# Gated weight tables kept in 32 bit and merged by one 32-bit product per block, with the splitting of their shares taken out of the first phase

## The reference

```python
gh = relu(einsum('bsd,hd->bsh', x, gfc1_w) + gfc1_b)
g = (einsum('bsh,eh->bse', gh, gfc2_w) + gfc2_b).mean(axis=1)     # 16 batches x 8 gates
W1m = W1 + einsum('be,efd->bfd', g, tv_W1)                        # tv_W1: 8 x 512 x 128
W2m = W2 + einsum('be,edf->bdf', g, tv_W2)                        # tv_W2: 8 x 128 x 512
h = relu(einsum('bsd,bfd->bsf', x, W1m) + b1m[:, None, :])
out = einsum('bsf,bdf->bsd', h, W2m) + b2m[:, None, :]
```

## Time and profile before

| | |
|---|---|
| median of three runs | 747.9 us |
| profiled execution, its own time | 749.55 us |
| span of its trace | 747.8 us |
| busy PE / PEld / DVE / ACT / POOL | 93% / 71% / 88% / 87% / 62% |
| matmuls | 12002 |
| mean granted clock of TensorE | 0.975 of full |
| first phase, loop part | about 70 to 440 us |
| blocks 0 to 7, 8 to 15, second group | 482 to 494, 496 to 505, 607 to 621 us |

### The profile page before, as it was taken

One profiled execution on the slowest core, in us unless ns is written; L12 is line 12 of the kernel. 1 busy time (PEld: TensorE's weight loads), 2 busy tenths in 40 slices (PEclk: granted clock), 3 DMA queues, 4 the chain that ended last, 5 costly groups with the idle time before them and its releaser, 6 DMA issues. The chain is left out here.

```text
span 747.8 us, 38168 instructions
## 1 busy us (share of the span) xinstructions
PE 692.5 (93%) x12002; PEld 533.8 (71%) x12002; DVE 659.1 (88%) x2409; ACT 649.1 (87%) x1780; POOL 465.2 (62%) x790
## 2 busy tenths in 40 slices
PE   4898899999999999999999999888999998999993
PEld 2576677777777777777777777775777787777772
DVE  5697889999999999999999999768898977998983
ACT  4797989999999999999999999557888876888883
POOL 3686778888888888888888888421333321333333
PEclk9798999999999999999999999899999999999998
DMA  4757676666666666666666666410222211222221
GB/s 149 112 110 134 132 129 129 148 143 131 148 142 132 148 141 132 148 141 134 148 139 135 148 142 123 74 51 1 73 85 83 71 58 31 85 70 84 84 84 70
DMA packets 202485, 82.66 MB, mean 111 GB/s; under 512 B 176093, under 2 KB 189824, under 8 KB 202377
## 3 DMA queue, kind: packets, MB, share of 16 engines
q1 hardware_dynamic: 202440, 82.08, 48.3%
HBM read 22.79 MB, written 17.30 MB: 54 GB/s over the span
## 5 line engine op out<-in xcount | busy, mean ns | idle before, releaser
L892 DVE SCALAR_TENSOR_TENSOR scores_lo<-p_a,scores_hi 128x512 f16<-128x512 f32 x256 | 173.3, 683 | 1.7 <-ACT scores_hi L786 1.3
L786 ACT ACTIVATE scores_hi<-p_a 128x512 f16<-128x512 f32 x256 | 156.2, 611 | 9.3 <-PE p_a L623 9.3
L1010 POOL CAST qk_parts<-qk_f 128x512 f16<-128x512 f32 x128 | 78.0, 610 | 50.2 <-issue 24.9
L1442 POOL TENSOR_TENSOR ffn_rstd_shift<-ffn_rstd_shift,consts 128x4 f32<-128x4 f32 x32 | 36.5, 1142 | 109.1 <-DVE ffn_rstd_shift L1400 109.1
L984 POOL TENSOR_TENSOR stats<-stats,consts 128x2 f32<-128x2 f32 (+1 forms) x128 | 88.2, 689 | 17.9 <-DVE stats L925 13.1
L1224 PE MATMUL psb<-merged_W_of_batch,h_hi 128*128 128x128 f16 x512 | 94.5, 220 | 2.2 <-DVE h_lo L1378 1.5
L1378 DVE TENSOR_TENSOR h_lo<-h_f,h_hi 128x512 f16<-128x512 f32 x128 | 95.6, 786 | 1.1 <-ACT h_hi L1280 1.1
L1269 ACT ACTIVATE h_f<-psb,merged_b_of_batch 128x512 f32<-128x512 f32 x128 | 87.2, 709 | 10.3 <-PE psb L1205 8.6
L1225 PE MATMUL psb<-merged_W_of_batch,h_hi 128*128 128x128 f16 x512 | 94.2, 220 | 0.0
L1226 PE MATMUL psb<-merged_W_of_batch,h_lo 128*128 128x128 f16 x512 | 94.1, 220 | 0.0
L1016 POOL TENSOR_TENSOR qk_parts<-qk_f,qk_parts 128x256 f16<-128x256 f32 x128 | 85.9, 671 | 10.2
(11 more groups left out here) (215 smaller groups left out, 2697.5 us busy)
## 6 DMA issues: line engine op xcount, KB each, us to landing
x_f<-in_x SPq DMA_DIRECT2D x32, 256.0 KB, 3.2
t_rows<-t SPq DMA_DIRECT2D x64, 128.0 KB, 1.8
t_back<-t_rows SPq DMA_DIRECT2D x32, 256.0 KB, 2.6
out<-out_tile SPq DMA_DIRECT2D x32, 256.0 KB, 2.1
tv_share<-in_L_ffn_tv_W SPq DMA_DIRECT2D x32, 128.0 KB, 2.2
qkT_parts<-qk_parts SPq DMA_TRANSPOSE x128, 3.1
zT_hi_lo<-z_parts SPq DMA_TRANSPOSE x128, 2.3
merged_W<-in_L_ffn_W SPq DMA_DIRECT2D x2, 256.0 KB, 4.4
```

The costliest lines, as they stand in the source:

```text
L786: nc.scalar.activation(ah[:, t % 2, cols], p_a[:, cols], ACT.Relu).then_inc(ahi_ready[eo], 1)
L892: nc.vector.scalar_tensor_tensor(al[:, t % 2, cols], p_a[:, cols], 0.0, ah[:, t % 2, cols], ALU.max, ALU.subtract).then_inc(alo_ready[eo], 1)
```

## The change

The two 16-bit halves of the tables become one 32-bit table `tv`. SP loads the shares straight to their place in it, both at t = 1 and without a wait. The stages `tv_hi` and `tv_lo` go. The gates are kept in 32 bit only, with the scale WS moved into the constant `delta`. Of the four products per output the three with table parts become one with 32-bit operands. Besides, `VECTOR_ORDER` has `stats2` ahead of `v_lo` and `mean_var2`, `mean_var1` ahead of `state_lo`, and `GPSIMD_ORDER` has `split_x` ahead of `z_hi`.

```diff
-                ("exp_qk", 1), ("state_hi", 3), ("v_hi", 1), ("tv_hi", 0), ("scores_hi_0", 4), ("copy_out", 6),
+                ("exp_qk", 1), ("state_hi", 3), ("v_hi", 1), ("scores_hi_0", 4), ("copy_out", 6),
-GPSIMD_ORDER = [("rsqrt", 1), ("z_hi", 10), ("split_x", 0), ("z_lo", 10), ("qk_hi", 2), ("qk_lo", 2),
+GPSIMD_ORDER = [("rsqrt", 1), ("split_x", 0), ("z_hi", 10), ("z_lo", 10), ("qk_hi", 2), ("qk_lo", 2),
...
-        tv = [sb(top, f"tv_{s}", [P, 2, FO * C], F16) for s in ("hi", "lo")]
+        tv = sb(top, "tv", [P, 2, FO * C])
...
-                        if t not in (1, 5) or isinstance(b, int) and b + 1 == B:
-                            return
-                        which = t // 4
-                        sp.wait_ge(ones_set, 1)
-                        sp.wait_ge(tv_split, TVP * b + TVP // 2 * (which + 1))
-                        tv_rows(b + 1, which)
...
+                        if t != 1 or isinstance(b, int) and b + 1 == B:
+                            return
+                        tv_rows(b + 1)
+
+                    def tv_rows(b):
+                        cols = bass.ds(b * TVW, TVW)
+                        for i, src in enumerate((d["L1_ffn_tv_W1"].rearrange("e (i o) d -> (e i) (o d)", i=FI),
+                                                 d["L1_ffn_tv_W2"].rearrange("e (i o) f -> (e i) (o f)", i=FI))):
+                            sp.dma_start(tv[:, i, cols], src[:, cols]).then_inc(tv_loaded, 16)
...
-                            mm(o, th, gh, start=True, stop=False)
-                            mm(o, th, gl, start=False, stop=False)
-                            mm(o, tl, gh, start=False, stop=False)
+                            mm(o, tv[:, 0, c0:c0 + P], g, start=True, stop=False)
                             last = mm(o, w1s[:, c0:c0 + P], delta2h[:, :, :].rearrange("p b i -> p (b i)"),
                                       start=False, stop=True)
...
-                        link(nc.vector.tensor_tensor(gbf[:, :, :], kcol("delta").unsqueeze(1).broadcast_to([P, GB, FI]),
-                                                     grep[:, GB:B].unsqueeze(2).broadcast_to([P, GB, FI]), ALU.mult))
-                        link(nc.vector.tensor_copy(gbh[:, GB:B, :], gbf[:, :, :]))
-                        nc.vector.tensor_tensor(gbl[:, GB:B, :], gbf[:, :, :], gbh[:, GB:B, :], ALU.subtract)\
+                        nc.vector.tensor_tensor(gb[:, GB:B, :], kcol("delta").unsqueeze(1).broadcast_to([P, GB, FI]),
+                                                grep[:, GB:B].unsqueeze(2).broadcast_to([P, GB, FI]), ALU.mult)\
                             .then_inc(gb_ready, 1)
```

More of the change, by code:

```diff
@@ L170, in build @@
         grep = sb(top, "gate_by_row", [P, B])
[L171 to L173 removed]
+        gb = sb(top, "gate_blocks", [P, B, FI])
         bw = wm1p[:, 1, 0:4 * BW].bitcast(F32).rearrange("p (i w) -> p i w", i=2)
@@ L420, in build @@
             qk_turned, z_turned = [[sem(f"{s}_{i}") for i in range(4)] for s in ("qk_turned", "z_turned")]
-            tv_loaded = [sem(f"tv_loaded_{i}") for i in range(2)]
-            tv_hi_ready, tv_split = sem("tv_hi_ready"), sem("tv_split")
+            tv_loaded = sem("tv_loaded")
             def at_least(eng, s, value):
@@ L508, in store @@
                             .then_inc(t1_stored[pair], 16)
-                    for which in range(2):
-                        tv_rows(0, which)
+                    tv_rows(0)
                     sp.wait_ge(base_stored, 32)
@@ L696, in merge_w1 @@
                             pe.wait_ge(base_placed, 16 * 4)
-                            pe.wait_ge(tv_split, TVP * B)
+                            pe.wait_ge(tv_loaded, 32 * B)
                             pe.wait_ge(gb0_ready, 1)
@@ L700, in merge_w1 @@
                             pe.wait_ge(mlo_ready, k - 1)
-                        gh, gl = [x[:, 0:GB, :].rearrange("p b i -> p (b i)") for x in (gbh, gbl)]
+                        g = gb[:, 0:GB, :].rearrange("p b i -> p (b i)")
                         for j in range(4):
@@ L731, in split_x @@
                         nc.scalar.activation(xh[:, hf, cols], xf[:, hf, cols], ACT.Copy).then_inc(xh_ready, 1)
-                    def tv_hi(b, t):
-                        if t % 2:
-                            return
[L736 to L741, removed]
                     def read_t1(b, t):
@@ L823, in merged_w1_hi @@
                             .then_inc(mhi_ready, 1)
-                    run(act, SCALAR_ORDER, {"tv_hi": tv_hi, "split_x": split_x, "read_t1": read_t1, "v_hi": v_hi,
+                    run(act, SCALAR_ORDER, {"split_x": split_x, "read_t1": read_t1, "v_hi": v_hi,
                         "exp_qk": exp_qk, "relu_qk": relu_qk,
@@ L842, in mean_var1 @@
                         nc.vector.bn_aggr(st[:, t % 4, MEAN:MEAN + 2], st[:, t % 4, 0:9]).then_inc(mv1, 1)
[L844 to L852, removed]
                     def v_lo(b, t):
@@ L964, in merged_w1 @@
                         nc.vector.tensor_tensor(lo, src, hi, ALU.subtract).then_inc(mlo_ready, 1)
-                    run(dve, VECTOR_ORDER, {"tv_lo": tv_lo, "stats1": stats1, "mean_var1": mean_var1, "v_lo": v_lo,
+                    run(dve, VECTOR_ORDER, {"stats1": stats1, "mean_var1": mean_var1, "v_lo": v_lo,
                         "make_qk": make_qk, "shift2": shift2, "state_lo": state_lo,
@@ L1181, in merge @@
                                     c0 = (4 * i + j) * C
-                                    th, tl, base = tv[0][:, 0, :], tv[1][:, 0, :], w1s
+                                    rows, base = tv[:, 0, :], w1s
                                 else:
                                     c0 = (4 * (i % 2) + j) * F + (i // 2) * P
-                                    th, tl, base = tv[0][:, 1, :], tv[1][:, 1, :], w2s
+                                    rows, base = tv[:, 1, :], w2s
                                 o = ps[:, merge_bank(g, k), j * P:(j + 1) * P]
-                                gh, gl = (x[:, g * GB:(g + 1) * GB, :].rearrange("p b i -> p (b i)")
-                                          for x in (gbh, gbl))
-                                mm(o, th[:, c0:c0 + P], gh, start=True, stop=False)
-                                mm(o, th[:, c0:c0 + P], gl, start=False, stop=False)
-                                mm(o, tl[:, c0:c0 + P], gh, start=False, stop=False)
+                                mm(o, rows[:, c0:c0 + P], gb[:, g * GB:(g + 1) * GB, :].rearrange("p b i -> p (b i)"),
+                                   start=True, stop=False)
                                 last = mm(o, base[:, c0:c0 + P], delta2h[:, :, :].rearrange("p b i -> p (b i)"),
```

22 lines of the change are left out of this document (5 added, 17 removed).

## The result

The kernel took 757.0 us after the change (median of 12 runs, 753.3 to 759.5), against 748.8 us before (12 runs, 745.7 to 751.7) on the same chip: 1.0100 times the time before, 95% interval 1.0077 to 1.0123. The forecast was 757 us: the same time, but from three runs of the kernel before with a median of 747.9 us; the forecast change was +9.1 us and the measured one is +8.2. The profiled span went from 747.8 to 754.9 us.

A forecast was written before the change was run, and what follows sets the result against it. SP's queue was taken to bound the first phase and PE the second group's merging. The terms 7.1 + 3.0 + 1.0 - 1.0 - 1.0 gave +9.1 us, 757 us; the range to hold 8 in 10 was 750 to 763 us.

The forecast's parts named there:

- What bounds the kernel: First phase: SP's queue, never waiting from 132 to 440 us, sets the 28 us turn; PE paces the second group's merging.
- Rival A: First phase: ACT and DVE set the pace, so removing tv_lo gains 22 us, giving 737 us; chance 0.06.
- Second group, +7.1 us: Merging of 16 blocks, paced by PE: 0.44 us more per block with the 32-bit product, all on the path.
- sixth unit: Merged output: L669's row gives 0.33 us, one unit beyond the five counted from the skill page (0.28 us), origin unknown.
- Blocks 8 to 15, +3.0 us: Merging of these eight blocks: +3.5 us for the product, less for two DVE gate steps of 0.23 + 0.29 us.
- Drain, +1.0 us: Blocks 0 to 7: +1.5 us for the product, partly filling PE's waits, less 0.5 us for two gate steps.
- the splits at the ends, -1.0 us: Ramp and drain: removing tv_hi and tv_lo gains 1 us, at most 6.7; nothing counts from 132 to 440 us.
- SP's queue, -1.0 us: SP's loads of table shares: between 0.1 us less and 0.15 us more each, -2.2 to +3.3 us over 11 batches.
- Rival D: Loads with both ends worked out at run time hold SP +0.3 us each, 8 us in all, 765 us; chance 0.05.
- The orders, 0: DVE's and POOL's changed orders give nothing under SP's pace, between -1 and +1 us at the ends.
- B: Rival: the 32-bit product is hidden, the merging adds under 2 us, no change at 748 us; chance 0.10.
- C: Rival: the merging costs more, 0.17 us per output (768 us) or 0.11 with nothing hidden (761 us); chance 0.09.

The follow-up runs named there:

- e4: Kernel after, with both tables loaded once by two 2 MB transfers that ScalarE issues ahead of the first phase: 752.1 us, ratio 1.0062.
- e5: Kernel before, with t1 stored once per half batch instead of twice, two SP issues fewer a turn: 747.3 us, ratio 0.9990.
- e10: Kernel after, with four 16-bit base products per output (tables' and gates' share left out) and t1 stored once per half batch: 732.5 us, ratio 0.9784.
- e12: Kernel before, with t1 stored once per half batch and ScalarE's tv_hi left out, upper halves cleared once: 747.2 us, ratio 0.9990.
- e8: Kernel after, with t1 stored once per half batch and the tables in eight 512 KB transfers from ScalarE: 745.8 us, ratio 0.9966.
- e6: Kernel after, with t1 stored once per half batch instead of twice: 742.8 us, ratio 0.9930.
- e7: Kernel after, with each merged block's four 32-bit products made first, then its four 16-bit base products: 751.0 us, ratio 1.0050.
- e3: Kernel before with all its splits, each output's three 16-bit table products replaced by one 32-bit product of constants: 760.3 us, ratio 1.0169.
- e2: Kernel after, with each merged output made by four 16-bit base products, the tables' and gates' share left out: 744.7 us, ratio 0.9957.
- e1: Kernel after, with VectorE's and GpSimd's orders of work set back to those of the kernel before: 754.5 us, ratio 1.0095.

## Why the prediction was right, step by step

**What bounds the kernel.** The queue's pace was read rightly for the kernel before and for the one after: 28.00 and 27.93 us a turn, no wait of SP in the loop, and e4's 1.20 us for 1.18 us of issues. The step was incomplete in one point and used two signs that don't hold. It took the full engines for stretched ones; e5 shows a second bound 0.08 us below the first, and e10 that the splits, with the orders, are worth 1.05 us a turn once the queue has room. The 15.0 us for which the scores sat idle were not the others being late on the queue: 13.3 us of them lie before 132 us and 0.4 in the loop. And a turn that repeats to 0.01 us is no sign of a queue: in e12 and e8, where SP waits and the engines set the pace, eleven turns in a row took 27.95 to 27.97 and 26.70 to 26.72 us, no less steady than under the queue. What carries the step is the missing wait of SP, and e4 and e6 tested it. Rival A's mechanism was real, at about 15 us instead of 22; it was shut off in both kernels by the queue, which is what the prediction said, and not by its own smallness.

**Second group, +7.1 us.** Measured 6.9: 0.333 against 0.223 us an output. The neighbourhood of L669 gave the price to 0.003 us, sixth unit included. e7 tells that the sixth unit went with the sequence of the two sorts. The Trainium skill, "FP8 and Floating Point Precision", section TensorE Precision Notes, counts four passes for true FP32; e7's 0.226 us against 0.055 agrees. An estimate by that page alone was 5.3 us for the 24 dense blocks, where 10.3 were measured (6.9 and 3.5 before rounding).

**Blocks 8 to 15, +3.0 us.** Measured 3.5, the full 8 x 0.44. The 0.5 us taken off for DVE's two steps on the gates wasn't on the path. They are gone in the kernel after (between 505.6 and 507 us DVE makes one step of 0.28 us, and then waits 0.44 us for ACT). e3, which keeps both steps, has the same 12.2 us, and the same 102.0 us in the half of the feed-forward behind them, 0.4 less than before. So the two stretches together cost +3.1 us, near the +3.0 of the sum, but by another way than it gave.

**Drain, +1.0 us, and the splits at the ends, -1.0 us.** The profiled pair shows +0.8 us for the drain with both in it, but at different clocks. Pairs whose drains have nearly the same granted clock part them. The product: e3 against before (0.94 in both) +2.2 us, e6 against e10 (0.97 in both) +1.8. The splits with the gate steps and orders: e2 against before (0.93 and 0.94) -1.8 us. Both together: after against e5 (0.91 in both) -0.6 us, so the splits are worth nearer 3 us there. Each of these is one profiled run against another. The product thus cost about 2 us in the drain where the prediction took 1.5, and the splits and gate steps gave 2 to 3 us where it took 1.5 in all. Both sizes were too small, and they nearly cancel. The 2.9 us of the ramp can't be called the change's: e3 and e5, whose ramp has before's work on the engines, ended the first turn at 102.0 and 101.9 us against 103.4, e1, e2 and e7 without splits at 101.4 to 102.3. By e2's interval the first phase as a whole gained 1.9 to 4.4 us.

**SP's queue, -1.0 us.** Measured -0.07 us a turn, 0.9 over 13 turns. (The twelve turns of the table are 0.2 us shorter in all, since the first of them, still in the ramp, took 28.6 us before and 29.1 after.) Rival D is out. **The orders, 0:** e1.

**B and C** fall with 0.333 us an output; nothing of the product was hidden in the dense blocks, and 64 outputs took no longer each than L669 had said.

The sum was +9.1 us against 8.2 measured. The parts as the runs give them are +10.3 for the dense blocks, -0.4 behind blocks 8 to 15, -0.9 in the loop and about -0.6 in the drain at equal clock, +8.4 us. The large term and the pace of the loop were right by their mechanism. That the time came out at 757.0 to the microsecond is luck: the change was put 0.9 us too high, and the twelve runs of the kernel before have a median 0.9 us above the three on which the forecast stood.

## What to carry to other kernels

Before an engine at 97 to 99% is called the bound, look at the queue that issues its transfers: if it never waits, take an issue off it and see whether the turn follows. Where it does, work taken off the engines comes back as waiting for transfers. A turn that repeats exactly says nothing about who sets it. Ask of a wait in which stretch it lies before it serves as evidence. When two bounds lie close together, a change that lifts one shows nothing until the other is lifted; try them together before judging either, as the square of runs does. A wait for a transfer may have begun at another transfer ahead of its issue, so follow it back one step. Price a new sort of instruction from a row with the same neighbours, and when sorts with different weight loads alternate, try them grouped.

## What the runs showed of the hardware that was not expected

- A 32-bit 128x128 product of 128 columns costs 0.226 us behind its like (e7) and 0.278 us behind a single 16-bit one (0.333 less 0.055, after), at full clock.
- A pipeline of engines that wait for each other can repeat as exactly as a queue that never waits: 27.95 to 27.97 us a turn in e12, 26.70 to 26.72 in e8.
- A store of 256 KB holds SP's queue no longer than one of 128 KB: 0.35 us in e6 as in the kernel after. Two issues fewer a turn, with twice the bytes in each, gave 1.05 us a turn.
- Large transfers of another queue delay small ones of SP's queue. Beside 4 MB of tables in e4 a store of SP's took 13.6 us to land, and SP, which waited 12.3 us for it, issued its first transpose 8.6 us late. Beside four transfers of 512 KB in e8's drain the transposes took up to 7.9 us to land instead of 2.3 to 3.2, and PE waited 3.6 us for one.
- tv_lo, two inputs in SBUF, took from 280 to 800 ns in the loop for the same 128x128 shape, in the kernel before, in e5 and in e12 alike. The Trainium skill, "SBUF — State Buffer", section Who interferes with whom, says that such an instruction and GpSimd's reads of SBUF shut each other out; the spread agrees, but POOL was not freed when tv_lo went: it was busy 237.1 us of 280 before, 234.3 after, and 238.2 in e1, which has no tv_lo and before's orders.
